# A routed-expert stage whose rows are added into DRAM in two halves of 512 columns instead of one transfer of 1024

## The reference, cut to what matters

```
x = x + xattn(layernorm(x), context, context)        # 32 query heads, 8 kv heads
x = x + (eta * read(layernorm(x)) + layernorm(x))    # read: softmax(max - x x^T) x
n = layernorm(x)
logits     = n @ gate_w                               # [1024 rows, 8 experts]
topv, topi = top_k(logits, 2)
w          = softmax(topv)
out        = x + sum over the 2 chosen experts e of  w_e * (n @ expert_w[e])
```

## Time and profile before

| | before |
|---|---|
| median of 3 runs | 1091.89 us |
| profiled execution: time | 1090.4 us |
| profiled execution: span | 1088.8 us |
| its mean granted clock of TensorE | 0.993 |
| PE busy | 1051.4 us, 97% |
| DVE, ACT, POOL busy | 631.8, 478.4, 243.3 us |
| mean data rate of the DMA engines | 174 GB/s |

### The profile page before, as it was taken

One profiled execution on the slowest core, in us unless ns is written; L12 is line 12 of the kernel. 1 busy time (PEld: TensorE's weight loads), 2 busy tenths in 40 slices (PEclk: granted clock), 3 DMA queues, 4 the chain that ended last, 5 costly groups with the idle time before them and its releaser, 6 DMA issues. The chain is left out here.

```text
span 1088.8 us, 25346 instructions
## 1 busy us (share of the span) xinstructions
PE 1051.4 (97%) x9020; PEld 960.8 (88%) x9021; DVE 631.8 (58%) x1624; ACT 478.4 (44%) x1129; POOL 243.3 (22%) x414
## 2 busy tenths in 40 slices
PE   8999989999999999999999999789998899999996
PEld 8999889999999999999999999567776688888885
DVE  6641246666666676666666667667888444354220
ACT  4321245555555555555545555523234244454331
POOL 2000201212112121212121121044455222322232
PEclk9999999999999999999999999899999999999999
DMA  9442566665657575665657664464538587578332
GB/s 342 137 154 80 183 187 171 182 186 175 197 166 209 159 196 162 193 178 175 194 174 201 213 176 122 153 213 94 108 81 278 155 243 252 156 238 251 108 76 37
DMA packets 78602, 189.45 MB, mean 174 GB/s; under 512 B 16512, under 2 KB 27136, under 8 KB 74400
## 3 DMA queue, kind: packets, MB, share of 16 engines
q1 hardware_dynamic: 64096, 154.15, 46.0%
q0 software_dynamic: 14400, 33.88, 13.2%
HBM read 148.66 MB, written 44.56 MB: 177 GB/s over the span
## 5 line engine op out<-in xcount | busy, mean ns | idle before, releaser
L483 ACT ACTIVATE prob<-bank,nmax 128x257 f32<-128x257 f32 x256 | 121.9, 476 | 244.2 <-DVE nmax L629 244.2
L629 DVE TENSOR_REDUCE nmax<-bank 128x1 f32<-128x257 f32 x256 | 108.9, 425 | 160.1 <-PE bank L844 160.1
L711 PE MATMUL bank<-cT_h,wkv_h 128*128 128x256 f32 x512 | 154.8, 302 | 0.0
L720 PE MATMUL bank<-wkv_h,cT_h 128*128 128x256 f32 x512 | 154.5, 302 | 0.0
L711 PE MATMUL bank<-cT_h,wkv_l 128*128 128x256 f32 x512 | 144.8, 283 | 0.0
L720 PE MATMUL bank<-wkv_h,cT_l 128*128 128x256 f32 x512 | 144.6, 283 | 0.0
L711 PE MATMUL bank<-cT_l,wkv_h 128*128 128x256 f32 x512 | 144.5, 282 | 0.0
L720 PE MATMUL bank<-wkv_l,cT_h 128*128 128x256 f32 x512 | 144.1, 282 | 0.0
L377 POOL DMA_DIRECT2D qcat<-q_scratch x128 | 70.2, 555 | 274.0 <-PE bank L844 270.9
L1691 PE MATMUL bank<-w_h,rows_h 128*128 x272 | 108.7, 400 | 0.0
L1691 PE MATMUL bank<-w_l,rows_h 128*128 x272 | 107.3, 394 | 0.0
(11 more groups left out here) (218 smaller groups left out, 2387.0 us busy)
## 6 DMA issues: line engine op xcount, KB each, us to landing
kcat<-k_scratch SPq DMA_DIRECT2D x128, 258.0 KB, 4.2
cx<-in_context SPq DMA_DIRECT2D x32, 1024.0 KB, 8.1
raw<-in_expert_w SPq DMA_DIRECT2D x48, 512.0 KB, 7.2
qcat<-q_scratch POOLq DMA_DIRECT2D x128, 128.0 KB, 3.2
k_scratch<-kT_h SPq DMA_DIRECT2D x32, 258.0 KB, 2.9
k_scratch<-kT_l SPq DMA_DIRECT2D x32, 258.0 KB, 3.1
x_in<-in_x SPq DMA_DIRECT2D x16, 512.0 KB, 7.2
expert_raw<-in_expert_w SPq DMA_DIRECT2D x16, 512.0 KB, 7.8
```

The lines of the kernel that those rows point to most:

```text
L483: act.activation(prob[1 - par][:, s, 0:SK], s_ps[s % 2][:, 0:SK], ACT.Exp, bias=nmax[:, 1 - par, s:s + 1], accum_out=sums[:, 1 - par, s:s ...
L629: dve.reduce_max(nmax[:, 1 - par, s:s + 1], s_ps[s % 2][:, 0:SK], AXX, negate=True).then_inc(max_done, 1)
L711: o = pe.matmul(k_ps[:, j * 256:(j + 1) * 256], wkv[w][:, k, j * P:(j + 1) * P], cT[t][:, b % 2, k, :], start=(j == 0 and k == 0 and n == ...
L720: o = pe.matmul(v_ps[:, a * KV:(a + 1) * KV], cT[t][:, b % 2, k, a * P:(a + 1) * P], wkv[w][:, k, KV:2 * KV], start=(a == 0 and k == 0 and ...
```

## The change

Each entry of the table of slots gets four numbers instead of two: row number, weight, and the numbers of the row's two halves, 2r and 2r+1. The output is seen as 2048 half rows of 512 columns. `scatter` issues two indirect transfers for a tile, each of 128 half rows: the first waits for half 0 of `acc` only, the second for half 1. The counts of the semaphore `written` double with it. The table in DRAM has 16 bytes an entry instead of 8, `no_tokens` 300 numbers a partition instead of 150, and POOL fills two more columns of `entries` (two more iota instructions) at the start.

```diff
--- before.py
+++ after.py
@@ -896,7 +896,7 @@
         xg = sb("xg", [P, 2, D], F32)
         yT = sb("yT", [P, KC, BT, GW], F32)
         tiles = sb("tiles", [1, 9, COLS], I32)
-        idx = sb("idx", [P, 4, 2], I32)
+        idx = sb("idx", [P, 4, 4], I32)
         eta_sb = sb("eta_sb", [P, 1], F32)
         stats2, stats3 = sb("stats2", [P, 2, 6], F32), sb("stats3", [P, 2, 6], F32)
         mean_var2, mean_var3 = sb("mean_var2", [P, 2], F32), sb("mean_var3", [P, 2], F32)
@@ -931,8 +931,8 @@
         ones = sb("ones", [P, P], F32)
         expert_iota = sb("expert_iota", [P, E], F32)
         region = sb("region", [P, E], F32)
-        entries = sb("entries", [P, 4 * NT], I32)
-        no_tokens = sb("no_tokens", [P, 2 * ROWS // P], I32)
+        entries = sb("entries", [P, 8 * NT], I32)
+        no_tokens = sb("no_tokens", [P, 4 * ROWS // P], I32)
         steps128 = sb("steps128", [P, E, NT], F32)
         over = sb("over", [P, E, NT], F32)
         n_tiles = sb("n_tiles", [P, E], F32)
@@ -1000,6 +1000,8 @@
             if rest:
                 from_tile(last - rest, (last - rest) % 4, rest)
 
+        half_rows = out.rearrange("t (h n) -> (t h) n", h=2)
+
         def fixed_rows(i):
             row = (0, B * SQ, P)[i]
             return slot_dram[row:row + P, :]
@@ -1023,7 +1025,7 @@
             for b in range(BT):
                 sp.dma_start(yT[:, :, b, SQ:GW], gate.rearrange("(c p) e -> p c e", p=P)).then_inc(small_loaded, 16)
             sp.dma_start(eta_sb[:, :], eta.rearrange("(a b) -> a b", a=1).to_broadcast([P, 1])).then_inc(small_loaded, 16)
-            sp.wait_ge(consts, 12)
+            sp.wait_ge(consts, 14)
             sp.dma_start(slot_dram.rearrange("(p n) o -> p (n o)", p=P), no_tokens[:, :]).then_inc(slots_cleared, 16)
             for c in range(KC):
                 load_first(0, c)
@@ -1063,17 +1065,19 @@
             pool.memset(probT[:, :], 0.0).then_inc(consts, 1)
             pool.memset(ones[:, :], 1.0).then_inc(consts, 1)
             pool.memset(before[:, :], 0.0).then_inc(consts, 1)
-            pool.iota(no_tokens[:, :], [[1, 2 * ROWS // P]], base=B * SQ, channel_multiplier=2 * ROWS // P).then_inc(consts, 1)
+            pool.iota(no_tokens[:, :], [[1, 4 * ROWS // P]], base=2 * B * SQ, channel_multiplier=4 * ROWS // P).then_inc(consts, 1)
             pool.memset(zero8[:, :], 0.0).then_inc(consts, 1)
             pool.iota(expert_iota[:, :], [[1, E]], base=0, channel_multiplier=0, allow_small_or_imprecise_dtypes=True).then_inc(consts, 1)
             pool.iota(region[:, :], [[B * SQ, E]], base=0, channel_multiplier=0, allow_small_or_imprecise_dtypes=True).then_inc(consts, 1)
-            pool.iota(entries[:, :].rearrange("p (t k c) -> p t k c", k=2, c=2)[:, :, :, 0], [[P, NT], [0, 2]], base=0,
-                      channel_multiplier=1).then_inc(consts, 1)
+            of_tile = entries[:, :].rearrange("p (t k c) -> p t k c", k=2, c=4)
+            pool.iota(of_tile[:, :, :, 0], [[P, NT], [0, 2]], base=0, channel_multiplier=1).then_inc(consts, 1)
+            for h in range(2):
+                pool.iota(of_tile[:, :, :, 2 + h], [[2 * P, NT], [0, 2]], base=h, channel_multiplier=2).then_inc(consts, 1)
             pool.iota(steps128[:, :, :], [[0, E], [P, NT]], base=0, channel_multiplier=0, allow_small_or_imprecise_dtypes=True).then_inc(consts, 1)
             pool.iota(tile_iota[:, :], [[1, COLS]], base=0, channel_multiplier=0, allow_small_or_imprecise_dtypes=True).then_inc(consts, 1)
             pool.memset(only[:, :], 0.0).then_inc(consts, 1)
             pool.memset(minus_half[:, :], -0.5).then_inc(consts, 1)
-            pool.wait_ge(consts, 12)
+            pool.wait_ge(consts, 14)
             pool.affine_select(out=earlier[:, :], in_=ones[:, :], compare_op=ALU.is_gt, fill=0.0, base=0,
                                pattern=[[1, P]], channel_multiplier=-1).then_inc(consts, 1)
             pool.memset(steps128[:, 1:E, 0:1], -1.0).then_inc(consts, 1)
@@ -1117,7 +1121,7 @@
                 pool.wait_ge(rows_ready, t + 1)
                 for c in range(2):
                     pool.indirect_dma_start(slot_dram, bass.IndirectOffsetOnAxis(ap=slot[:, 2 * t + c:2 * t + c + 1], axis=0),
-                                            entries[:, 4 * t + 2 * c:4 * t + 2 * c + 2], None).then_inc(scattered, 16)
+                                            entries[:, 8 * t + 4 * c:8 * t + 4 * c + 4], None).then_inc(scattered, 16)
 
             def first_row(i):
                 e = entry(pool, i, 0, E - 1)
@@ -1143,10 +1147,12 @@
                                         bounds_check=tokens - 1, oob_is_err=False).then_inc(xg_loaded[place % 2], 16)
 
             def scatter(i, place):
-                wait_apart(pool, acc_ready, 2 * i + 2, passed)
-                tokens = tokens_of(i)
-                pool.indirect_dma_start(out[0:tokens, :], bass.IndirectOffsetOnAxis(ap=idx[:, place, 0:1], axis=0), acc[:, place % 2, :], None,
-                                        bounds_check=tokens - 1, oob_is_err=False, compute_op=ALU.add).then_inc(written[place % 2], 16)
+                halves = 2 * tokens_of(i)
+                for h in range(2):
+                    wait_apart(pool, acc_ready, 2 * i + h + 1, passed)
+                    pool.indirect_dma_start(half_rows[0:halves, :], bass.IndirectOffsetOnAxis(ap=idx[:, place, 2 + h:3 + h], axis=0),
+                                            acc[:, place % 2, h * 512:(h + 1) * 512], None, bounds_check=halves - 1, oob_is_err=False,
+                                            compute_op=ALU.add).then_inc(written[place % 2], 16)
 
             for t in range(NT + 2):
                 if on(t, 1):
@@ -1173,12 +1179,12 @@
             pool.wait_ge(gT_done, 4)
             gather(3, 3)
             scatter(0, 0)
-            pool.wait_ge(written[0], 16)
+            pool.wait_ge(written[0], 32)
             load_idx(4, 0).then_inc(idx_loaded, 16)
             scatter(1, 1)
             pool.wait_ge(gT_done, 6)
             gather(4, 0)
-            pool.wait_ge(written[1], 16)
+            pool.wait_ge(written[1], 32)
             load_idx(5, 1).then_inc(idx_loaded, 16)
             scatter(2, 2)
 
@@ -1187,7 +1193,7 @@
                 par = place % 2
                 pool.wait_ge(gT_done, 2 * i + 2)
                 gather(i + 2, (place + 2) % 4)
-                wait_apart(pool, written[1 - par], 8 * (i + par), passed)
+                wait_apart(pool, written[1 - par], 16 * (i + par), passed)
                 load_idx(i + 3, (place + 3) % 4).then_inc(idx_loaded, 16)
                 scatter(i, place)
             used = pool.value_load(tiles[0:1, 4, 0:1], min_val=E - 1, max_val=MT)
@@ -1196,7 +1202,7 @@
             pool.wait_ge(idx_loaded, used * 16 + 16 * 3)
             for p in range(2):
                 pool.wait_ge(xg_loaded[p], every_scatter[p] + 16)
-                pool.wait_ge(written[p], every_scatter[p])
+                pool.wait_ge(written[p], every_scatter[p] * 2)
 
         @block.scalar
         def _(act):
@@ -1249,10 +1255,10 @@
 
             def scale_rows(i, place, h):
                 if known(i) and i < 2:
-                    act.wait_ge(consts, 16)
+                    act.wait_ge(consts, 18)
                     act.wait_ge(x2_ready, 2 * NT - 2 + 2 * i)
                 else:
-                    act.wait_ge(written[place % 2], 8 * (i - place % 2))
+                    act.wait_ge(written[place % 2], 16 * (i - place % 2))
                 act.wait_ge(y_done, 2 * i + h + 1)
                 act.activation(acc[:, place % 2, h * 512:(h + 1) * 512], y_ps[place % 2][h][:, :], ACT.Identity, bias=zero8[:, 0:1],
                                scale=idx[:, place, 1:2].bitcast(F32)).then_inc(acc_ready, 1)
@@ -1381,7 +1387,7 @@
 
                 dve.wait_ge(egap_ready, t + 1)
                 chain(dve.tensor_scalar(denom[:, :], egap[:, :], 1.0, None, ALU.add))
-                weight = [entries[:, 4 * t + 2 * k + 1:4 * t + 2 * k + 2].bitcast(F32) for k in range(2)]
+                weight = [entries[:, 8 * t + 4 * k + 1:8 * t + 4 * k + 2].bitcast(F32) for k in range(2)]
                 chain(dve.reciprocal(weight[0], denom[:, :]))
                 dve.tensor_tensor(weight[1], egap[:, :], weight[0], ALU.mult)
                 dve.wait_ge(rank_done, t + 1)
@@ -1395,7 +1401,7 @@
             def turn_shares(t):
                 par = t % 2
                 if t == 0:
-                    dve.wait_ge(consts, 16)
+                    dve.wait_ge(consts, 18)
                     dve.wait_ge(small_loaded, 16 * (BT + 1))
                 dve.wait_ge(g_done, t + 1)
                 dve.tensor_reduce(low[:, :], g_ps[:, 0:SQ], AXX, ALU.min).then_inc(low_ready, 1)
@@ -1563,7 +1569,7 @@
 
             def mix(t):
                 if t == 0:
-                    pe.wait_ge(consts, 16)
+                    pe.wait_ge(consts, 18)
                 pe.wait_ge(probT_ready, t + 1)
                 for h in range(2):
                     if t >= 1:
```

(2 more changed lines are left out.)

## The result

| | before | after |
|---|---|---|
| median of 10 runs each | 1092.22 us | 1095.49 us |
| lowest to highest | 1089.63 to 1095.33 | 1094.40 to 1100.01 |
| ratio after / before | | 1.0042, 95% interval 1.0025 to 1.0059 |
| span of the profiled execution | 1088.8 us | 1098.4 us |
| its mean granted clock | 0.993 | 0.987 |

The changed kernel is 4.6 us slower by the ratio. The time of 1095.49 lies inside the forecast range of 1089.8 to 1096.0; the forecast of "no change" was wrong. In a later set on one chip the same changed kernel came out level, 0.9997 (0.9977 to 1.0016).

The account below looks back on a forecast made before the run. PE, busy 97% of the span, was taken as the bound, leaving only its waits and the last landing. Last transfer -0.95, early tiles +1.5, clearing +0.05, slots 0 gave +0.6 on 1091.89: 1092.5 us, range 1089.8 to 1096.0.

Parts of the forecast that it names:

- no change: Whole kernel: time within 0.2%, or 2.2 us, of before; chance 0.62.
- the early tiles: Tiles 0 to 2, where POOL is late: doubled scatters delay later gathers and cost PE +1.5 us, ends 0 and +4.0.
- the slots: Scatters of slot entries: 16 bytes instead of 8 changes nothing, 0 us, ends -1 and +1.
- lands 6.2 later ... just in time: Gather of tile 5: issued at 887.6, lands at 893.8, before PE wants it at 894.4.
- +0.5 for tiles 5 and 6: Gathers of tiles 5 and 6: added PE loss for zero margin and landings differing by more than 1 us.
- The slower rival: POOL from scatter 0 to tile 6's gather: halves land no sooner than wholes, PE loses 4.0; 1095.9 us, chance 0.28.
- Tile 4: PE's wait before turning tile 4: 0.8 to 2 us instead of 0.28.
- The end: Last scatter: its second half lands sooner with half the data, -0.95 us, ends 0 and -1.9.
- the faster rival: Scatters: a half costs as little as an almost empty tile, landing 4.5; sum -2.8, 1089.1 us, chance 0.10.
- The clearing: Clearing the table at the start: 150 KB instead of 75 costs +0.05 us, ends 0 and +0.7.
- The sum: All terms: -0.95 + 1.5 + 0.05 + 0 = +0.6 us, giving 1092.5.

Follow-up runs that it names:

- table_only: The kernel before with only the wider table of slots (16-byte entries), each scatter still one whole transfer; 0.9955 of before.
- after_again: The changed kernel unaltered, run in a later set for a second profile; 0.9997 of before.
- gather_between: The changed kernel with the gather of tile 5 issued on POOL between the two halves of tile 2; 0.9996 of before.
- thin_weights: The changed kernel with the weights of experts 3 to 7 loaded in 16 of 1024 columns only, output not the reference's; 0.9940 of before.
- wide32_late_halves: The changed kernel with 32-byte entries, tiles 0 to 3 scattered whole and halves from tile 4 on; 0.9931 of before.
- filler_early: The kernel before with 16-byte entries and whole scatters, plus five small POOL writes ahead of each scatter of tiles 0 to 3; 1.0042 of before.
- halves_together: The changed kernel with both halves of a tile waiting for both halves of acc; 1.0019 of before.
- early_whole: The changed kernel with tiles 0 to 3 each scattered in one transfer, halves from tile 4 on; 0.9950 of before.

## Why the prediction was wrong

Two terms of the sum were far off, with opposite signs: the early tiles, forecast at +1.5 and measured at +4.8, whose step "lands 6.2 later ... just in time" failed and which made the kernel slower; and the slots, forecast at 0 and measured at -4.9.

*The slots: the term that was mis-sized most.* The prediction put the change from 8 to 16 bytes at 0, ends -1 and +1, arguing that a scatter of 4 KB rows lands in 6.9, "so size is not what makes this slow". Size is not; distance is, and no row could show it. Measured with table_only: -4.9 us. In the profiles the stage is 3.0 us shorter than before; PE's wait for tile 2 goes from 3.56 or 1.41 to 0.2 to 0.6. The remaining 2 us between ratio and stage are inside the ratio's interval of 2.7 to 7.2 us.

*The early tiles: right in the issue, wrong in the landing.* The gather of tile 5 was forecast 3.96 us later than before. Counted from PE's turning of tile 2 it went out at 23.4 us before (883.64 - 860.26), 27.1 in after_again (884.30 - 857.21) and 28.8 in after: 3.7 and 5.4 later. The step that failed is the next, "lands 6.2 later ... just in time": it kept the landing of the earlier trace rows for a transfer moved by 4 us, and there the weights of expert 3 are loading. It took 9.2 and 9.7. Rather than +0.5 for tiles 5 and 6 PE lost 2.5 and 4.2, and then 1.5 and 1.6 to the clock, which the sum did not have at all. In all the early tiles cost 4.8 us in after_again (1.07 + 2.50 + 1.5 - 0.28) where +1.5 stood, and the ends, 0 to +4.0, did not hold it. The slower rival had POOL's late start reach PE, which is right, but at tiles 4 and 6 and for another reason: it wanted halves that land no sooner than wholes. That its time of 1095.9 lies 0.4 us from the measured 1095.49 is luck, since it had neither the gain of the table nor the meeting with the weights.

*Tile 4.* Forecast wait 0.8 to 2; measured 1.59 and 1.07. Right in these two profiles; the 0.25 and 0.51 of gather_between and thin_weights, with the same list up to there, show how wide it scatters.

*The end.* The landing of the last half was forecast at 5.3 to 5.6; it is 4.4 in after_again, about the 4.5 that the faster rival took from an almost empty whole tile. That does not mean that half the data costs nothing: the second half of that same almost empty tile, issued at 1059.87 in after_again, lands sooner still (DMA view):

```profile
out_x<-acc,idx POOLq DMA_INDIRECT x1, 3.3
```

So the data of a full half cost about 1.1 us (4.4 - 3.3), of a whole tile 1.9 (6.4 - 4.5): 0.8 saved, near the 0.95 forecast. The other 1.2 of the 2.0 us is that a half without data lands in 3.3 where a whole without data took 4.5, which the forecast had as equal; why, no run shows. But the half of the last tile is issued 0.9 us later than assumed, so the end gained 0.9 and 1.1 against 0.95 forecast: right by two errors.

*The clearing.* +0.05 forecast, within ends to +0.7. Measured 3.12 and 2.91 us against 2.72 and 2.81: +0.1 to +0.4, small in any case.

*The sum.* With measured terms: -4.9 (table, clearing included), +4.8 (early tiles), -1.0 (end) gives -1.1 for after_again, measured -0.3, give or take 2 us. The first set's +4.6 is not reproduced by that sum. Its profile has 2.2 us more of waits at tiles 4 and 5 than after_again and the 3.1 us ahead of tile 1; whether its ten runs had either as a rule is not known, since one was profiled and that was the slowest. This stays open.

## What to carry to other kernels

Where one engine issues transfers in order, an added issue costs nothing when the engine waits anyway and delays everything behind it when it is late; split a transfer only where its issuer has slack, which here was from tile 4 on. A transfer that moves by some microseconds must be priced at the traffic of its new place, not with its old landing; look at which bulk load starts there. And when a table of small entries is written by scatter, test a wider entry by itself: here padding from 8 to 16 bytes was worth more than the change that brought it along.

## What the runs showed of the hardware

- Scatters of 128 small entries into DRAM landed in a median of 7.0 and 7.2 us with entries 8 bytes apart, 4.5 to 5.0 at 16 bytes, and 2.2 to 2.3 at 32. Writing only 8 of 16 bytes gave 4.8, the same as writing all. The Trainium skill, "DMA: Bandwidth & Descriptors", specifications, says that transfers below 512 bytes are done as read-modify-write; all these entries are below that, so it does not tell 8 bytes from 32, and no run here shows it. Why the distance counts, no run shows either.
- An adding scatter of 128 half rows of 2 KB landed in 4.4 to 5.4 us in the quiet stretch behind 1015 us, 128 rows of 4 KB in 6.0 to 6.5; of almost empty tiles the halves took 3.3 to 3.7 and the whole rows 4.3 to 4.5. Beside the loading of weights halves took up to 10.3 (gather_between) and whole rows up to 10.4 (wide32_late_halves).
- Behind waits of PE of 2.50 to 4.20 us in the expert stage (after, after_again, gather_between) the granted clock fell for a few microseconds and the next tile took 1.5 to 1.6 us longer; behind 3.61 us in filler_early it was 2.8 us, with one window at 0.50, the lower level (1.2 GHz) throughout. Behind 1.32 us (halves_together) and behind 3.56 us at tile 2 in before it did not fall. Length alone does not decide it.
- The building of an indirect transfer grew from 1.6 to up to 2.6 us while DVE split weights, for scatters too (2.48 in gather_between above, 2.64 in wide32_late_halves).
- POOL started the last half 1.79 or 1.80 us after ACT's end in all four profiles whose early tiles are in halves and whose last half waits for its own half alone (after, after_again, gather_between, thin_weights), but 0.88 after it in early_whole and wide32_late_halves, whose loop is the same code. In the chain of waits the difference is one stretch of "issue" on POOL, 1.43 us in after_again and 0.52 in early_whole. What fills it is not known.
